# First message stage of a graph kernel: the edge-feature product on 64 rows per tile, both tiles of a pair into two PSUM banks

## The reference, cut to what matters

```python
h_src = node_features[src]
h_dst = node_features[dst]
msg_in = jnp.concatenate([h_src, h_dst, edge_features], axis=-1)
h = jax.nn.silu(msg_in @ msg_W1 + msg_b1)
messages = h @ msg_W2 + msg_b2
aggregated = jax.ops.segment_sum(messages, dst, num_segments=...)
```

## Time and profile before

| | us |
|---|---|
| median of three runs | 13495.78 (13480.02 to 13504.6) |
| the profiled execution | 13491.28 |
| its span, first to last instruction | 13489.7 |
| first message stage in it | about 6025 to 8490 |

### The profile page before, as it was taken

One profiled execution on the slowest core, in us unless ns is written; L12 is line 12 of the kernel. 1 busy time (PEld: TensorE's weight loads), 2 busy tenths in 40 slices (PEclk: granted clock), 3 DMA queues, 4 the chain that ended last, 5 costly groups with the idle time before them and its releaser, 6 DMA issues. The chain is left out here.

```text
span 13489.7 us, 226628 instructions
## 1 busy us (share of the span) xinstructions
PE 9118.6 (68%) x54949; PEld 7335.8 (54%) x54950; DVE 8174.9 (61%) x20048; ACT 4331.8 (32%) x13907; POOL 9126.6 (68%) x9951
## 2 busy tenths in 40 slices
PE   4466666655555558879999999877777776444444
PEld 2255555544444437768888888554545465333333
DVE  6677777744444436657777777477777744333334
ACT  6633223211111115543333333455555532000002
POOL 9977777777777773356666666177777713777775
PEclk9987777765555559999999999999999977555555
DMA  5023333322222228857777777322222221122224
GB/s 194 0 41 49 49 49 50 49 60 75 74 74 74 73 63 277 279 172 198 197 197 197 197 196 189 66 56 56 56 56 56 56 25 53 52 53 53 52 53 57
DMA packets 2004093, 1307.44 MB, mean 97 GB/s; under 512 B 1477267, under 2 KB 1755599, under 8 KB 2003970
## 3 DMA queue, kind: packets, MB, share of 16 engines
q1 hardware_dynamic: 1679682, 604.85, 19.3%
q0 software_dynamic: 324288, 701.18, 19.0%
HBM read 939.12 MB, written 372.83 MB: 97 GB/s over the span
## 5 line engine op out<-in xcount | busy, mean ns | idle before, releaser
L1125 POOL DMA_INDIRECT edge_fs<-tab_a,edge_ix x1664 | 1575.7, 947 | 957.7 <-DVE edge_ix L1220 633.8
L2070 POOL DMA_INDIRECT edge_ys<-tab,edge_ix x1664 | 1579.9, 949 | 903.9 <-issue 506.8
L657 POOL DMA_INDIRECT by_src<-send_row,send_pl x1664 | 1678.5, 1009 | 515.6 <-issue 506.5
L1616 POOL DMA_INDIRECT edge_sv<-tab,edge_ix x1664 | 1592.5, 957 | 572.8 <-issue 427.5
L480 POOL DMA_INDIRECT records<-place_pl,place_place x1568 | 1606.6, 1025 | 516.7 <-issue 476.7
L2114 PE MATMUL edge_psA<-edge_ys,edge_oh 128*128 128x128 f32 x3328 | 861.2, 440 | 1259.1 <-DMA edge_ys<-tab,edge_ix 1238.5
L2114 PEld LDWEIGHTS edge_psA<-edge_ys,edge_oh 128*128 128x128 f32 x3328 | 740.8, 328 | 1379.5 <-issue 1128.1
L1731 PE MATMUL edge_psA<-edge_oh,edge_m 128*128 128x128 f32 x6656 | 951.3, 302 | 580.5 <-DVE edge_m L1712 580.2
L1731 PEld LDWEIGHTS edge_psA<-edge_oh,edge_m 128*128 128x128 f32 x6656 | 870.7, 211 | 651.2 <-DVE agg L1671 623.0
L2103 DVE TENSOR_TENSOR agg<-agg,edge_psA 128x128 f32 x1664 | 476.9, 287 | 1233.8 <-PE edge_psA L2114 1232.5
L1268 PE MATMUL edge_psH<-edge_fd,edge_ohT 128*128 128x256 f32 x3328 | 1021.6, 389 | 27.1 <-issue 19.7
(11 more groups left out here) (345 smaller groups left out, 24233.5 us busy)
## 6 DMA issues: line engine op xcount, KB each, us to landing
edge_fd<-tab_b SPq DMA_DIRECT2D x1664, 128.0 KB
max_row<-by_src SPq DMA_DIRECT2D x392, 256.0 KB, 3.9
running<-max_back POOLq DMA_DIRECT2D x392, 256.0 KB
records<-count_tmpl SPq DMA_DIRECT2D x64, 858.0 KB, 20.1
send_pl<-records SPq DMA_DIRECT2D x416, 132.0 KB, 2.4
edge_pl<-records SPq DMA_DIRECT2D x832, 50.0 KB
place_pl<-in_edge_attr SPq DMA_DIRECT2D x390, 100.0 KB
by_src<-send_row,send_pl POOLq DMA_INDIRECT x1664, 2.2
```

Of the source, the lines that this page charges most:

```text
L657: pool.indirect_dma_start(S.by_src[:], bass.IndirectOffsetOnAxis(ap=at, axis=0), row[b][:, k, :], None, bounds_check=bound, oob_is_err=Fal ...
L1125: pool.indirect_dma_start(rows[b % len(rows)][:, k, :], None, table[:], bass.IndirectOffsetOnAxis(ap=ix[b][:, k:k + 1], axis=0)).then_inc( ...
L1616: pool.indirect_dma_start(sv[b % NSV][:, k, :], None, S.tab_2[:], bass.IndirectOffsetOnAxis(ap=ix[b % NSV][:, k:k + 1], axis=0)).then_inc( ...
L2070: pool.indirect_dma_start(ys[b][:, k, :], None, table, bass.IndirectOffsetOnAxis(ap=ix[b][:, k:k + 1], axis=0)).then_inc(s_got[b], 16)
```

## The change

For the edge product, `we` becomes 128 rows by 256 columns without zeros: rows 0 to 50 for tile 0, rows 64 to 114 for tile 1. A tile's product reads only its own 64 rows of eT and of `we`. First both tiles' one-hot products are formed, then both edge products. The two tiles' sums go to two banks (psH has 1024 columns now, tile 1 at column 512), twice double-buffered, so four banks. To make room, psT and psE share a bank. Each tile's edge product counts s_H, so that those who wait for it wait for two per pair.

```diff
-        we = ph.sb("we", [P, G2, H])
-        psT = [ph.bank(f"psT{k}", BF16) for k in range(2)]
-        psE = [ph.bank(f"psE{k}") for k in range(2)]
-        psH = [ph.bank(f"psH{k}") for k in range(2)]
+        we = ph.sb("we", [P, H])
+        psX = [ph.bank(f"psX{k}") for k in range(2)]
+        psT = [bank[:].bitcast(BF16)[:, 512:512 + G2 * P] for bank in psX]
+        psE = [bank[:, 0:P] for bank in psX]
+        psH = [ph.ctx.enter_context(nc.psum_tensor(f"edge1_psH{k}", [P, 1024], F32)) for k in range(2)]
...
-                wait(sp, s_H[o], n)
+                wait(sp, s_H[o], 2 * n)
...
-                    v.wait_ge(s_H[b], r + 1)
+                    v.wait_ge(s_H[b], 2 * r + 2)
                     v.wait_ge(s_got[b], (r + 1) * 16 * G2)
-                    rows = fs[b % NB][:].rearrange("p k c -> p (k c)")
-                    v.tensor_tensor(rows, psH[b % 2][:, :], rows, ALU.add).then_inc(s_in[b], 1)
+                    rows = fs[b % NB][:]
+                    both = psH[b % 2][:].rearrange("p (k c) -> p k c", k=G2)[:, :, 0:H]
+                    v.tensor_tensor(rows, both, rows, ALU.add).then_inc(s_in[b], 1)
...
-                    wait(act, s_H[o], n)
+                    wait(act, s_H[o], 2 * n)
...
                     for k in range(G2):
-                        c = slice(k * H, (k + 1) * H)
-                        e = slice(k * P, (k + 1) * P)
-                        pe.matmul(psH[b % 2][:, c], ohT[b % 2][:, e], fd[b % 2][:, k, :], start=True, stop=False)
-                        last = pe.matmul(psH[b % 2][:, c], eT[b % 2][:], we[:, k, :], start=False, stop=True)
-                    last.then_inc(s_H[b], 1)
+                        pe.matmul(psH[b % 2][:, 512 * k:512 * k + H], ohT[b % 2][:, k * P:(k + 1) * P], fd[b % 2][:, k, :],
+                                  start=True, stop=False)
+                    for k in range(G2):
+                        e = slice(EP * k, EP * (k + 1))
+                        pe.matmul(psH[b % 2][:, 512 * k:512 * k + H], eT[b % 2][e, :], we[e, :],
+                                  start=False, stop=True).then_inc(s_H[b], 1)
```

More of the change, by code:

```diff
@@ L1181, in _ @@
             for k in range(G2):
-                sp.dma_start(we[EP * k:EP * k + NE, k, :], a.L1_gnn_msg_W1[2 * D:2 * D + NE, :]).then_inc(s_w, 16)
-                sp.dma_start(we[EP * k + NE:EP * k + NE + 1, k, :], a.L1_gnn_msg_b1.rearrange("(a d) -> a d", a=1)).then_inc(s_w, 16)
+                sp.dma_start(we[EP * k:EP * k + NE, :], a.L1_gnn_msg_W1[2 * D:2 * D + NE, :]).then_inc(s_w, 16)
+                sp.dma_start(we[EP * k + NE:EP * k + NE + 1, :], a.L1_gnn_msg_b1.rearrange("(a d) -> a d", a=1)).then_inc(s_w, 16)
             at = []
@@ L1245, in step @@
                     act.wait_ge(s_T[b], r + 1)
-                    wait(act, s_H[o], n)
-                    act.activation(ohT[b % 2][:], psT[b % 2][:, 0:G2 * P], ACT.Copy)
-                    act.activation(eT[b % 2][:], psE[b % 2][:, 0:P], ACT.Copy).then_inc(s_TT[b], 1)
+                    wait(act, s_H[o], 2 * n)
+                    act.activation(ohT[b % 2][:], psT[b % 2], ACT.Copy)
+                    act.activation(eT[b % 2][:], psE[b % 2], ACT.Copy).then_inc(s_TT[b], 1)
                 else:
@@ L1276, in step @@
                         pe.transpose(psT[b % 2][:, k * P:(k + 1) * P], ohb[b % 2][:, k, :], S.ident_b[:])
-                    last = pe.transpose(psE[b % 2][:, 0:P], pl[b % NB][:].rearrange("p k c -> p (k c)"), S.ident[:])
+                    last = pe.transpose(psE[b % 2], pl[b % NB][:].rearrange("p k c -> p (k c)"), S.ident[:])
                     last.then_inc(s_T[b], 1)
```

## The result

The changed kernel takes 13422.44 us (median of four runs, 13414.16 to 13436.8) against 13492.13 us of the kernel before, run beside it: a ratio of 0.9949, 95% interval 0.9932 to 0.9967, or about 70 us less: half a per cent, and clear of 1. The forecast was 83 us more. The profiled execution's span is 13435.2 us.

What follows compares the result with a forecast made beforehand. TensorE was taken to bound the first message stage; 0.20 + 0.12 - 0.215 = +0.10 us per pair, times 832, gave +83 us, 13579 us. The range ran from 13317 less some 12 us up to 13666.

Steps and rivals of the forecast that it cites:

- What bounds the kernel: First message stage: TensorE bounds it, 2.96 us per pair, and a shorter or longer psH part moves the turn one to one.
- The price of the switch: Around the edge products: entering the 64-row form costs 0.20 us per pair, going back 0.12.
- the return after the 48-column transpose: Second message stage: the next 128x128 product's weight load showed no wait, so going back might cost zero.
- What runs side by side: Edge products: tile 1's first pass runs beside tile 0's second, four passes in three steps, 0.215 us less per pair.
- rival E: Edge passes pair up fully, two hidden, 0.43 us; with switches -0.12 to -0.23 per pair, 13305 to 13399 us; chance 0.05.
- sign of being wrong: Turns between 7000 and 8000 us growing by less than 0.03 us, or shrinking; the switch price would then have failed.
- The doubled count of s_H: Waits after psH: two counts per pair add nothing, since all who wait still wait for the last pass.
- Two banks for VectorE's addition: VectorE reading psH in two runs of 256 costs nothing that matters, with 0.52 us per pair of waiting before it.
- rival D: Edge products: row halves cost no switch, the hidden pass is all gain, -179 us, 13317 us; chance 0.18.

Runs made afterwards that it cites:

- experiment 4: Changed kernel with each edge product cut into two of 128 columns, tile 0's two, then tile 1's two: 13432.76 us, ratio 0.9955 to the kernel before.
- experiment 2: Changed kernel with both edge products reading rows 0 to 63, so tile 1's sums are wrong: 13746.89 us, ratio 1.0188 to the kernel before.
- experiment 5: Changed kernel with only tile 1's edge product counting s_H and all waits for one per pair: 13401.44 us, ratio 0.9932 to the kernel before.
- experiment 3: Changed kernel in the old order, one-hot and edge product of tile 0, then of tile 1: 14053.29 us, ratio 1.0416 to the kernel before.
- experiments 1: Changed kernel with edge products reading all 128 rows again, zeros in the other tile's half: 13509.06 us, ratio 1.0009 to the kernel before.

## Why the prediction was wrong, step by step

*What bounds the kernel:* right. TensorE bounds the stage before and after. That the turn moves one to one with the psH part was not: that part got 0.124 us shorter (0.432 less 0.191, 0.104 and 0.013), the turn 0.088, and the rest went into late starts.

*The price of the switch:* right, and near in size. In: 0.20 forecast, 0.19 measured. Out: 0.12 taken, 0.10 measured. The page named there holds for rows as well: the Trainium skill, "TensorEngine Tiling (Array Packing)", "Key Properties", has the array drained when the mode changes, and the traces agree with 0.09 us between the end of streaming and the next weight load, on the way in and on the way out. That the return after the 48-column transpose cost nothing would then be the case without a change of form; no run tests it.

*What runs side by side:* this step failed. The forecast let one of four passes be hidden, 0.215 us, on the ground that all rows showed matmuls starting in the program's order, so that tile 1's first pass would stay behind tile 0's second. But every product in those rows uses all 128 rows of the array, so none of them could have gone ahead; the rows couldn't bear that conclusion. Experiment 4 shows that passes on the other half don't wait for their turn, and experiment 2 that it takes another half. Two passes were hidden, 0.43 us. The Trainium skill, "TensorE: Matmul & The Clock Gate", part 3, "The mechanism", has products in different row groups start some 4 ns apart; here it is 7 ns at the median, and 13 in experiment 4. That starts keep the program's order, as the same section says, the starts in experiment 4 contradict, or at least the order in which the kernel issues its products.

By the steps as they stand, 0.19 + 0.10 - 0.43 = -0.14 us per pair, rival E with its switches, to which the prediction gave 0.05 and which it put below 13399 us. The measured time lies 23 us above that. The prediction's sign of being wrong came true, as the turns shrank, but it named the price of the switch as the step that would then fail; the price held, and the overlap failed.

*What was missing:* 0.036 us per pair of late starts, 30 us, and 0.013 by which the halves start apart, 11 us; with them the sum is -0.09 us per pair, 73 us less, and 70 were measured. The doubled count of s_H, which the prediction put down at nothing because nobody waits for anything else, cost 0.020 of it on ScalarE (experiment 5): the event is the same, but who waits goes on later. The rest goes with the load of fd, which ends more waits in a shorter turn; some of that went with the double count too, since experiment 5 took off 0.030. The prediction hid this load behind a turn that it expected to grow.

*Two banks for VectorE's addition:* right; its mean is 690 ns against 691, and a bank for psT and psE together delays the copy by nothing (0.316 us in experiment 5 as before).

*Sign and range:* the sign was wrong. That the time lies within the range is luck: the range reached below 13492 us for rival D, row halves without a switch, and the switch was paid.

*The arithmetic:* 0.20 + 0.12 - 0.215 is 0.105, which makes 87 us and not 83, and some rivals are counted from 13491.28 us and others from 13495.78. Neither changes a reading.

## What to carry to other kernels

Two products on different halves of the array's rows ran fully side by side here, all their passes, as neighbours in the program (experiment 3 has them apart, and nothing is hidden) and into different banks (one bank for both was not run); for that, one entry and one return have to be paid, here 0.30 us together, so the hidden streaming has to be longer than this, and products must be put together so that the form changes as seldom as possible. When a turn gets shorter, read again what ended the wait of its first instruction: here a wait on a later copy than needed and a load that is issued late took back part of the gain. Mending both, with the single count, brought another 75 us, as much as the change itself. And a pattern seen in a trace says nothing on cases in which it could not have been otherwise.

## What the runs showed of the hardware

- A pass of an f32 product over 64 rows and 256 columns takes 0.216 us like one over 128 rows (experiment 2); two on different halves start 6 to 7 ns apart, and so do the next two, 0.32 us later (the changed kernel).
- Into the 64-row form and out of it, the weight load starts 0.09 us after the last pass has streamed and isn't hidden: 0.33 us of idle weight loads at each of four switches a turn (experiment 3). With the open load a switch costs 0.19 us where f32 weights follow and 0.10 where bf16 weights do.
- Passes of one half don't wait behind passes of the other that stand ahead of them in the program (experiment 4).
- A wait for twice the round, in place of the round, put ScalarE's next instruction 0.08 us later in a quarter of the turns, always at the same two of eight places (experiments 1 and 5).
- Two counts of one semaphore from passes that start 6 to 7 ns apart: the second update stands 0.026 us later than a single one does (0.426 against 0.400 us behind the last pass's start, the changed kernel against experiment 5).
- At two of eight places in the ring, TensorE's first weight load stood 0.20 us behind the update that it waited for, elsewhere 0.042 (the changed kernel and the one before).
